# Row sums of an attention kernel by VectorE's block transpose and a spread through DRAM, in place of products with ones and reciprocals in PSUM

## The chip, the cores and the metric

The kernel runs on one core of a Trainium2 chip. The metric is the device time of the whole kernel in microseconds, lower is better; the time before is the median of three runs.

## The reference

One transformer block on 2048 tokens of width 128, in float32: layer norm with a conditioned scale and shift, attention of 16 heads of width 64 over all 2048 positions of a head, a second norm, and a mixture of 8 experts (top 2) with a shared one. The change touches the attention alone:

```python
xq = jnp.einsum('bsh,oh->bso', x, wq)       # and xk, xv
xq = xq.reshape(bsz, N_HEADS, seqlen, HEAD_DIM)
scores = jnp.einsum('bhid,bhjd->bhij', xq, xk) * SCALE
scores = jax.nn.softmax(scores, axis=-1)
out = jnp.einsum('bhij,bhjd->bhid', scores, xv)
out = out.reshape(bsz, seqlen, N_HEADS * HEAD_DIM)
return jnp.einsum('bso,ho->bsh', out, wo)
```

The reshape is plain, so each head reads 128 tokens and has 2048 positions of its own. The softmax needs the sum of the exponentials of each row, which is what the change computes in another way.

## The kernel before

**Units.** A unit is one head and one half of its 2048 query positions (`HALF` = 1024); there are 32 (`UNITS`), halves 0 and 1 of each head in turn. In a unit the scores stand transposed, keys on the partitions and 1024 queries on the columns, one tile of 128 keys at a time, 16 tiles (`kt`). TensorE makes a tile's scores in two PSUM banks (six products, `scores`, L1342 to L1348), ScalarE turns them into exponentials in one of 8 buffers `probs` (L918), TensorE multiplies these with the values (`weigh`, L1366) into one bank, and POOL adds the exponentials of all tiles (`add`, L1003, L1009) in two chains, `acc` and `acc_odd`, 14 additions of 128x1024, and merges the two in a fifteenth (L995). The total still has to be summed over its 128 partitions, for each of 1024 queries.

**Peaks.** The softmax subtracts for each query block a shift, from the maxima of products made ahead of time: for each unit 16 pairs (`pair`, L1289 on TensorE) are made while an earlier unit runs. All go to the same two PSUM banks (6 and 7), one after another, and TensorE waits for `peak_free` before each. VectorE reduces a pair to its maxima from PSUM (L1079), but for pairs 1, 3, ... 13 (`TAKEN`): these ScalarE copies to `peak_copy` (L860) and VectorE reduces the copy two places later (L1089). Then a small product turns the maxima (`turn_shift`), VectorE keeps them (L1097), and SyncE sends them by DMA (L742).

**The order by hand.** A unit has 8 steps of 4 places, so 32 places. In each step places 0 and 1 are the scores of two tiles, places 2 and 3 the value products of two earlier ones. Behind each place every engine runs the jobs that `side_jobs` puts there, in the same order on each engine: the next head's projections (`LONG_JOBS`: q, k, v), their remainders (`LOW_PLACES`), pairs 4 to 15 at places 1, 3, ... 23 (so pair 10 at place 13 and pair 11 at place 15) and pairs 0 to 3 of a later unit at places 25 to 31. Each engine's queue is served in order.

**Row sums and scaling.** "sum" (place 6 in half 0, 10 in half 1): two products of ones with the total, in the job bank (`sum_unit`, L1379), give each query's sum on all 64 partitions of a head. "inv": four reciprocals of 128 columns, PSUM to PSUM (`invert`, L1105). "scale": `scale_outputs` (L1112) multiplies the values' product `o_raw` (ScalarE's copy, L870) with them into `oT`. "out" (half 0, place 22): the head's output projection (`project`, L1392) and the residual sum on VectorE (`add_head`, L1118). The last unit's sum is made in the experts' part (`LAST_SUM`).

**SyncE's queue** holds, in a unit of half 0, the DMAs that swap the two 64-partition halves of `k_hi` behind each k (places 14 and 18), those of the differences behind "low k" (places 16 and 20) and the shift's (place 26); in half 1 the shift's alone.

**The end.** At places 17 and 27 to 31 of the last head, VectorE makes the remainders of expert weights from two SBUF tensors (L1178) and small steps of the norm (L366, L582, L583); the experts follow.

## Time and profile before

| | |
|---|---|
| median of three runs | 1318.63 us |
| the profiled execution's time | 1317.36 us |
| its span | 1315.6 us |
| TensorE busy | 1297.5 us, 99% |
| POOL busy | 1176.0 us, 89% |
| VectorE busy | 911.3 us, 69% |
| ScalarE busy | 888.3 us, 68% |
| granted TensorE clock | 0.999 |

The span runs from the first to the last instruction of one execution; the execution's own time is a little longer. A busy TensorE is not one at its peak, since the ends of its matmuls are modelled. The shares are means over attention (about 44 to 1228 us) and the experts behind it.

### The profile page before, as it was taken

To read this page: it belongs to the slowest core of one execution; us is meant where nothing else is said; L and a number is where in the kernel's file an instruction comes from. 1 tells how busy PE (TensorE), PEld (TensorE's weight loads), DVE (VectorE), ACT (ScalarE), POOL (GpSimd) and SP (SyncE) were. 2 spreads that over 40 slices of the span, in tenths; PEclk is the share of its full clock that TensorE was granted. 3 is DMA by queue.
4 is the path that set the end of the run, shared out by engine and by line. 5 is a ranking of instruction groups with operands and counts; after the bars stand their busy time and mean duration, and the time that the engine had idled before them with its cause. 6 is when DMAs were issued, how large, how long until landed. Compare 5 with 4: busy or idle time off the path is not lost. (4 is left out here: it accounts for less than half of the span.)

```text
span 1315.6 us, 22284 instructions
## 1 busy us (share of the span) xinstructions
PE 1297.5 (99%) x8792; PEld 705.3 (54%) x8792; DVE 911.3 (69%) x1036; ACT 888.3 (68%) x1096; POOL 1176.0 (89%) x538
## 2 busy tenths in 40 slices
PE   7999999999999999999999999999999999999998
PEld 5545545454555545454555555454545545454787
DVE  6767667676767677677767676776767676859575
ACT  6666767676766766666766666676767667775474
POOL 2499999999999999999999999999999999999644
PEclk9999999999999999999999999999999999999999
DMA  8010202020110202020100202020200102001323
GB/s 210 11 39 1 49 1 49 1 49 1 27 24 1 49 1 49 1 49 1 38 13 1 49 1 49 2 49 0 49 1 10 40 1 49 1 1 30 101 73 89
DMA packets 31962, 41.55 MB, mean 32 GB/s; under 512 B 4298, under 2 KB 15186, under 8 KB 31858
## 3 DMA queue, kind: packets, MB, share of 16 engines
q1 hardware_dynamic: 31714, 40.13, 12.5%
q8 instruction: 69, 1.13, 0.4%
q14 instruction: 35, 0.29, 0.1%
q10 hardware_dynamic: 144, 0.00, 0.0%
HBM read 13.70 MB, written 1.11 MB: 11 GB/s over the span
## 5 line engine op out<-in xcount | busy, mean ns | idle before, releaser
L918 ACT ACTIVATE probs<-ps 128x1024 f32<-128x1024 f32 x512 | 498.7, 1032 | 78.7 <-PE ps L1348 75.9
L1079 DVE TENSOR_REDUCE peak_parts<-ps 128x2 f32<-128x1024 f32 x297 | 362.2, 1223 | 236.8 <-PE ps L1289 235.1
L1366 PE MATMUL ps<-probs,v_sb 128*64 128x512 f32 x2048 | 522.8, 606 | 0.0
L1009 POOL TENSOR_TENSOR acc<-acc,probs 128x1024 f32<-128x1024 f32 x192 | 457.7, 2384 | 31.2 <-ACT probs L918 29.6
L1009 POOL TENSOR_TENSOR acc_odd<-acc_odd,probs 128x1024 f32<-128x1024 f32 x192 | 459.5, 2393 | 0.0
L860 ACT COPY peak_copy<-ps 128x1024 f32<-128x1024 f32 x215 | 218.6, 1017 | 242.0 <-PE ps L1289 168.0
L1089 DVE TENSOR_REDUCE peak_parts<-peak_copy 128x2 f32<-128x1024 f32 x215 | 260.7, 1212 | 34.2 <-ACT peak_copy L860 34.2
L1366 PEld LDWEIGHTS ps<-probs,v_sb 128*64 128x64 f32 x2048 | 123.8, 136 | 157.3 <-issue 118.4
L1342 PE MATMUL ps<-q_hi,d_swap_hi 64*128 64x512 f32 x512 | 201.4, 393 | 0.4 <-ACT probs L918 0.4
L1342 PE MATMUL ps<-q_hi,d_hi 64*128 64x512 f32 x512 | 201.5, 394 | 0.0
L1348 PE MATMUL ps<-q_hi,d_swap_lo 64*128 64x512 f32 x512 | 200.7, 392 | 0.0
L1348 PE MATMUL ps<-q_hi,d_lo 64*128 64x512 f32 x512 | 200.7, 392 | 0.0
L1345 PE MATMUL ps<-q_lo,d_hi 64*128 64x512 f32 x512 | 199.8, 390 | 0.0
L1345 PE MATMUL ps<-q_lo,d_swap_hi 64*128 64x512 f32 x512 | 199.7, 390 | 0.0
L1289 PE MATMUL ps<-k_hi,q_hi 64*128 64x512 f32 x512 | 120.3, 466 | 2.7 <-DVE peak_parts L1079 2.6
L1289 PE MATMUL ps<-k_swap_hi,q_hi 64*128 64x512 f32 x512 | 117.4, 454 | 1.3 <-DVE peak_parts L1079 1.1
L1289 PEld LDWEIGHTS ps<-k_hi,q_hi 64*128 64x128 f32 x512 | 47.7, 183 | 129.4 <-DVE peak_parts L1079 65.7
L1289 PEld LDWEIGHTS ps<-k_swap_hi,q_hi 64*128 64x128 f32 x512 | 47.6, 183 | 125.4 <-DVE peak_parts L1079 54.4
L1105 DVE RECIPROCAL ps<-ps 128x128 f32<-128x128 f32 x128 | 113.3, 930 | 0.0
L1345 PEld LDWEIGHTS ps<-q_lo,d_hi 64*128 64x128 f32 x512 | 94.7, 185 | 13.2
L1342 PEld LDWEIGHTS ps<-q_hi,d_swap_hi 64*128 64x128 f32 x512 | 95.0, 186 | 11.1 <-ACT probs L918 0.9
L1348 PEld LDWEIGHTS ps<-q_hi,d_lo 64*128 64x128 f32 x512 | 94.5, 185 | 11.7
(237 smaller groups left out, 1571.6 us busy)
## 6 DMA issues: line engine op xcount, KB each, us to landing
k_swap_hi<-k_hi SPq DMA_DIRECT2D x64, 128.0 KB, 2.3
d_swap_hi<-d_hi SPq DMA_DIRECT2D x64, 128.0 KB, 2.3
d_swap_lo<-d_lo SPq DMA_DIRECT2D x64, 128.0 KB, 2.3
q_hi<-weights_dram SPq DMA_DIRECT2D x8, 256.0 KB, 3.2
q_lo<-weights_dram SPq DMA_DIRECT2D x8, 256.0 KB, 4.6
k_hi<-weights_dram SPq DMA_DIRECT2D x8, 256.0 KB, 5.9
k_swap_hi<-weights_dram SPq DMA_DIRECT2D x8, 256.0 KB, 5.3
probs<-in_L_ffn_w_dram SPq DMA_DIRECT2D x2, 512.0 KB, 5.9
```

What stands on the lines that cost most here:

```text
L860: act.copy(peak_copy[:, :, :], ps[:, PEAK_BANK:PEAK_BANK + 2, :]).then_inc(peak_free, 1)
L918: act.activation(probs[:, kt % PROBS, :], ps[:, 2 * place:2 * place + 2, :].rearrange("p a b -> p (a b)"), ACT.Exp, scale=SCALE).then_inc( ...
L1009: pool.tensor_tensor(total, total, probs[:, kt % PROBS, :], ALU.add).then_inc(added, 1)
L1079: dve.tensor_reduce(peak_parts[:, :, i // STRETCHES, i % STRETCHES], ps[:, bank:bank + 2, :], AX.X, ALU.max).then_inc(peak_free, 1)
L1089: dve.tensor_reduce(peak_parts[:, :, i // STRETCHES, i % STRETCHES], peak_copy[:, :, :], AX.X, ALU.max).then_inc(copy_read, 1)
L1105: dve.reciprocal(job.ps[:, cols], job.ps[:, cols]).then_inc(part_inverted, 1)
L1289: mm = pe.matmul(ps[:, bank + b, :], q_hi[at, target_parity, q:q + P], keys[at, target_parity, cols], start=True, stop=True, tile_position ...
L1342: pe.matmul(ps[:, slot + b, :], hi[b][at[b], p, cols], q_hi[at[b], p, q], start=kt < 2, stop=False, tile_position=(b * HEAD_DIM, 0), skip_ ...
L1345: pe.matmul(ps[:, slot + b, :], hi[b][at[b], p, cols], q_lo[at[b], p, q], start=False, stop=False, tile_position=(b * HEAD_DIM, 0), skip_g ...
L1348: mm = pe.matmul(ps[:, slot + b, :], lo[b][at[b], p, cols], q_hi[at[b], p, q], start=False, stop=kt >= 2, tile_position=(b * HEAD_DIM, 0), ...
L1366: mm = pe.matmul(ps[at:at + HEAD_DIM, PV_BANK, :], v_sb[:, p, chunk_of(kt) * HEAD_DIM:(chunk_of(kt) + 1) * HEAD_DIM], probs[:, kt % PROBS, ...
```

## The change

The products with ones and the PSUM reciprocals go, but for the last unit. In their place, for each unit done, at places of the next unit that are the same in both halves:

- place 8, "turn sum": VectorE transposes the total (128x1024) in blocks of 32x32 into `k_raw`;
- place 10, "add sum": it sums over 32 neighbouring columns, 128x1024 to 128x32 (`sum_parts`): now each of four partition groups holds the part of its 32 keys rows for all 1024 queries;
- place 12, "fold": a block transpose of 128x32, four copies that bring the four groups to 32 partitions, a reduction over the four, a reciprocal of 32x32;
- SyncE (`spread_sums`, in its queue at place 12) writes the 1024 reciprocals to DRAM, waits until they have landed, and reads them back with two DMAs that repeat a row on 64 partitions;
- place 20 (28 in the last unit), "scale": VectorE multiplies `o_raw` with them, both in SBUF.

The scratch for it is the unit's own `acc` half. "out" moves from place 22 of half 0 to place 14 of half 1. New waits: ScalarE before its copy into `k_raw` (`sums_added`) and before its copy of the values' product (`out_scaled`), POOL before the first addition of a unit and TensorE before the projection (`out_scaled`), VectorE before the scaling (`sums_spread`). The diff, with one line of context at each place; left out are the lines that allocate `sum_parts` and the six semaphores.

```diff
@@ -39,8 +39,8 @@
 LONG_JOBS = (
-    {2: ("q", 0), 6: ("sum", 0), 14: ("k", 0), 18: ("k", 1), 22: ("out", 0), 26: ("shift", 0)},
-    {2: ("q", 1), 6: ("v", 0), 10: ("sum", 0), 19: ("v", 1), 26: ("shift", 0)},
+    {2: ("q", 0), 14: ("k", 0), 18: ("k", 1), 26: ("shift", 0)},
+    {2: ("q", 1), 6: ("v", 0), 14: ("out", 0), 19: ("v", 1), 26: ("shift", 0)},
 )
@@ -48,13 +48,11 @@
 INVERSES = 4
-SCALE_PLACES = (
-    {6: ("inv", 0), 7: ("inv", 1), 8: ("inv", 2), 10: ("inv", 3), 11: ("scale", 0)},
-    {11: ("inv", 0), 12: ("inv", 1), 13: ("inv", 2), 15: ("inv", 3), 16: ("scale", 0)},
-)
-
-COUNTED = ("q", "k", "v", "sum", "shift")
-JOBS_PER_HEAD = 10
+SUM_PLACES = {8: ("turn sum", 0), 10: ("add sum", 0), 12: ("fold", 0)}
+SCALE_PLACE, LATE_SCALE_PLACE = 20, 28
+
+COUNTED = ("q", "k", "v", "shift")
+JOBS_PER_HEAD = 8
 
@@ -81,11 +79,11 @@
 
-def side_jobs(half, sums=True, project=True, pairs=True, early=True, last_head=False, before_last=False):
+def side_jobs(half, sums=True, outs=True, project=True, pairs=True, early=True, last_head=False, before_last=False):
 
     for place, (kind, i) in LONG_JOBS[half].items():
-        if sums if kind in ("sum", "out") else pairs if kind == "shift" else project:
+        if outs if kind == "out" else pairs if kind == "shift" else project:
             places[place].append((kind, i))
@@ -102,8 +100,9 @@
     if sums:
-        for place, job in SCALE_PLACES[half].items():
+        for place, job in SUM_PLACES.items():
             places[place].append(job)
+        places[LATE_SCALE_PLACE if last_head and half == 1 else SCALE_PLACE].append(("scale", 0))
     if before_last:
@@ -236,7 +238,7 @@
         def jobs_at(t):
-            return PROLOGUE_JOBS if isinstance(t, int) and t == 0 else t * (2 * JOBS_PER_HEAD) + (PROLOGUE_JOBS - 1)
+            return t * (2 * JOBS_PER_HEAD) + PROLOGUE_JOBS
 
@@ -276,7 +278,8 @@
                     final_head = last and p == 1
-                    plan = side_jobs(half, sums=not (first and p == 0 and half == 0), project=not final_head,
+                    plan = side_jobs(half, sums=not (first and p == 0 and half == 0), outs=not (first and p == 0),
+                                     project=not final_head,
                                      pairs=not (final_head and half == 1), early=not final_head,
@@ -305,6 +308,19 @@
         TAIL_PAIRED = 7
+
+        sums_dram = nc.dram_tensor("sums_dram", [2, HALF], F32, kind="Internal").ap()
+
+        class SumParts:
+
+            def __init__(self, unit_done):
+                total = acc[:, unit_done % 2, :]
+                self.turned = k_raw[:, P:P + HALF]
+                self.spread = total[:, 0:BANK]
+                self.parts_turned = total[:, BANK:BANK + 32]
+                self.quarters = total[0:32, BANK + 128:BANK + 256].rearrange("p (g i) -> p g i", g=4)
+                self.sums = total[0:32, BANK + 256:BANK + 288]
+                self.inverse = total[0:32, BANK + 288:BANK + 320]
 
@@ -744,6 +760,17 @@
 
+            def spread_sums(unit_done):
+
+                parts = SumParts(unit_done)
+                sp.wait_ge(sums_inverted, unit_done + 1)
+                row = sums_dram[unit_done % 2:unit_done % 2 + 1, :]
+                sp.dma_start(row.rearrange("a (j i) -> (a j) i", j=32), parts.inverse).then_inc(sums_out, 16)
+                sp.wait_ge(sums_out, 16 * (unit_done + 1))
+                for b in range(2):
+                    sp.dma_start(parts.spread[b * HEAD_DIM:(b + 1) * HEAD_DIM, :],
+                                 row[:, b * BANK:(b + 1) * BANK].broadcast_to([HEAD_DIM, BANK])).then_inc(sums_spread, 16)
+
             def swap(parity, i, src, dst, signal):
@@ -779,6 +806,8 @@
                             for kind, i in jobs:
+                                if kind == "fold":
+                                    spread_sums(unit - 1)
                                 if kind == "k":
@@ -829,13 +858,15 @@
                 keep_setup(n)
-            def side(job, kind, i, parity):
+            def side(job, kind, i, parity, sums_before=0):
 
                     if kind == "k":
+                        if sums_before:
+                            act.wait_ge(sums_added, sums_before)
                         act.copy(k_raw[:, P + i * BANK:P + (i + 1) * BANK], job.ps).then_inc(raw_ready, 1)
@@ -860,13 +891,10 @@
 
-            sums = []
-
-            def copy_pv(unit_done, sum_before):
+            def copy_pv(unit_done):
                 act.wait_ge(pv_done, PAIRS * unit_done)
-                if sum_before is not None:
-
-                    act.wait_ge(job_free, sum_before)
+                if unit_done > 1:
+                    act.wait_ge(out_scaled, unit_done - 1)
                 act.copy(o_raw[:, :], ps[:, PV_BANK, :]).then_inc(o_copied, 1)
@@ -921,14 +949,12 @@
                                 if kind in COUNTED:
-                                    side(Job(jobs_at(t) + local), kind, i, 1 - p)
+                                    side(Job(jobs_at(t) + local), kind, i, 1 - p, unit)
                                 if kind == "step k":
                                     take_pair(i, target * PEAK_PAIRS + i, target)
-                                if kind == "sum":
-                                    sums.append(jobs_at(t) + local + 1)
                                 if kind in ("turn", "logits", "weights"):
@@ -943,10 +969,10 @@
                         if step == 0 and not first:
-                            copy_pv(unit, sums[-1] if sums else None)
+                            copy_pv(unit)
 
             pairs_of_heads(body)
-            copy_pv(UNITS, sums[-1])
+            copy_pv(UNITS)
             ffn_act(act)
@@ -997,8 +1023,9 @@
                     pool.wait_ge(exped, unit * TILES + (kt + 2))
+                    if n == 1 and unit > 1:
+                        pool.wait_ge(out_scaled, unit - 1)
                     if n == 2 and unit > 0:
-
                         pool.wait_ge(added, unit * ADDS)
@@ -1107,9 +1134,39 @@
 
-                dve.wait_ge(part_inverted, unit_done * INVERSES)
+                dve.wait_ge(part_inverted, INVERSES)
                 dve.wait_ge(o_copied, unit_done)
                 dve.tensor_tensor(oT[:, half_done, :], o_raw[:, :], job.ps, ALU.mult).then_inc(job_free, 1)
+
+            def turn_sum(unit_done, half_done):
+
+                dve.wait_ge(added, unit_done * ADDS + ADDS)
+                dve.transpose(SumParts(unit_done).turned, acc[:, half_done, :]).then_inc(sums_turned, 1)
+
+            def add_sum(unit_done):
+
+                parts = SumParts(unit_done)
+                dve.wait_ge(sums_turned, unit_done + 1)
+                dve.tensor_reduce(sum_parts[:, :], parts.turned.rearrange("p (j r) -> p j r", r=32), AX.X,
+                                  ALU.add).then_inc(sums_added, 1)
+
+            def fold_sums(unit_done):
+
+                parts = SumParts(unit_done)
+                dve.wait_ge(sums_added, unit_done + 1)
+                link(dve.transpose(parts.parts_turned, sum_parts[:, :]))
+                for g in range(4):
+                    ins = dve.tensor_copy(parts.quarters[:, g, :], parts.parts_turned[32 * g:32 * g + 32, :])
+                link(ins)
+                link(dve.tensor_reduce(parts.sums, parts.quarters.rearrange("p g i -> p i g"), AX.X, ALU.add))
+                dve.reciprocal(parts.inverse, parts.sums).then_inc(sums_inverted, 1)
+
+            def scale_unit(unit_done, half_done):
+
+                dve.wait_ge(sums_spread, 32 * (unit_done + 1))
+                dve.wait_ge(o_copied, unit_done + 1)
+                dve.tensor_tensor(oT[:, half_done, :], o_raw[:, :], SumParts(unit_done).spread,
+                                  ALU.mult).then_inc(out_scaled, 1)
 
@@ -1160,10 +1217,14 @@
                                     low_k(Job(jobs_at(t) + (local - 1)), i, 1 - p, head * 2 + (3 + i))
-                                if kind == "inv":
-                                    invert(i, Job(jobs_at(t) + (local - 1)))
+                                if kind == "turn sum":
+                                    turn_sum(unit - 1, 1 - half)
+                                if kind == "add sum":
+                                    add_sum(unit - 1)
+                                if kind == "fold":
+                                    fold_sums(unit - 1)
                                 if kind == "scale":
-                                    scale_outputs(Job(jobs_at(t) + (local - 1)), unit, 1 - half)
+                                    scale_unit(unit - 1, 1 - half)
                                 if kind == "out":
@@ -1385,6 +1446,7 @@
                 pe.wait_ge(job_free, job.earlier)
+                pe.wait_ge(out_scaled, min(2 * head + 2, UNITS - 1))
                 for half in range(2):
@@ -1451,8 +1513,6 @@
                                     pair(i, (unit + 2) * PEAK_PAIRS + i, head + 1, 1 - p, half, PEAK_BANK)
-                                if kind == "sum":
-                                    sum_unit(job, unit - 1, 1 - half)
                                 if kind == "out":
```

## Rows read from the trace of the kernel before

**Rows 1.** The page, part 1: busy us (share of the span) xinstructions:

```profile
PE 1297.5 (99%) x8792; PEld 705.3 (54%) x8792; DVE 911.3 (69%) x1036; ACT 888.3 (68%) x1096; POOL 1176.0 (89%) x538
```

**Rows 2.** Busy time by stretch, two units of attention:

```profile
core 0: us, PE busy (x) PEld busy (x) DVE busy (x) ACT busy (x) POOL busy (x), PEclk, DMA share, GB/s
154.00:228.00 74.00, 74.00 (x516) 38.52 (x514) 50.85 (x53) 50.95 (x60) 71.07 (x32) 1.00 0.10 22
```

**Rows 3.** Groups by line: busy us, mean ns of one, idle before:

```profile
L860 ACT COPY peak_copy<-ps 128x1024 f32<-128x1024 f32 x215 | 218.6, 1017 | 242.0 <-PE ps L1289 168.0 <-DVE peak_parts L1089 74.0
...
L1105 DVE RECIPROCAL ps<-ps 128x128 f32<-128x128 f32 x128 | 113.3, 930 | 0.0
...
L1379 PE MATMUL ps<-acc,ones 128*64 128x512 f32 x128 | 32.9, 593 | 0.0
...
L1112 DVE TENSOR_TENSOR oT<-o_raw,ps 128x512 f32<-128x512 f32 x32 | 22.0, 687 | 1.1
```

**Rows 4.** Waits: engine line, waited for: us in total, times, longest:

```profile
PEld ps L1289 <- DVE peak_parts L1079: 120.1, 166, 1.9
```

**Rows 5.** Timeline of TensorE in a unit of half 1 (start us, us):

```profile
533.77 1.03 PE L1379 MATMUL ps<-acc,ones 128*64 128x512 f32 x4
534.63 1.03 PE L1366 MATMUL ps<-probs,v_sb 128*64 128x512 f32 x4
...
537.31 0.40 PE L1289 MATMUL ps<-k_swap_hi,q_hi 64*128 64x512 f32 x2
...
539.50 0.51 PE L1289 MATMUL ps<-k_swap_hi,q_hi 64*128 64x512 f32 x2
```

**Rows 6.** Timeline of VectorE, same unit:

```profile
534.12 1.21 DVE L1089 TENSOR_REDUCE peak_parts<-peak_copy 128x2 f32<-128x1024 f32 x1
535.24 1.77 DVE L1105 RECIPROCAL ps<-ps 128x128 f32<-128x128 f32 x2
```

**Rows 7.** Timeline of POOL, same unit:

```profile
535.70 2.40 POOL L1009 TENSOR_TENSOR acc_odd<-acc_odd,probs 128x1024 f32<-128x1024 f32 x1
538.15 2.38 POOL L1009 TENSOR_TENSOR acc<-acc,probs 128x1024 f32<-128x1024 f32 x1
540.47 2.40 POOL L1009 TENSOR_TENSOR acc_odd<-acc_odd,probs 128x1024 f32<-128x1024 f32 x1
```

**Rows 8.** Timelines of VectorE and POOL at the norm's small steps:

```profile
1141.79 0.21 DVE L366 RECIPROCAL rstd<-std 128x12 f32<-128x12 f32 x1
...
1142.03 0.62 DVE L582 TENSOR_TENSOR shift_ln<-mean_var,rstd 128x12 f32<-128x12 f32 x1
...
1142.56 2.42 POOL L1009 TENSOR_TENSOR acc_odd<-acc_odd,probs 128x1024 f32<-128x1024 f32 x1
...
1142.69 2.33 DVE L583 TENSOR_SCALAR shift_ln<-shift_ln 128x12 f32<-128x12 f32 x1
```

**Rows 9.** Timeline of VectorE and POOL at the weight remainders:

```profile
1182.86 7.58 DVE L1178 TENSOR_TENSOR w_lo<-w1T,k_hi 128x384 fp32r<-128x384 f32 x3 [5.31 <-ACT k_hi L938]
...
1190.11 2.55 POOL L1003 TENSOR_TENSOR acc<-probs 128x1024 f32<-128x1024 f32 x1
1190.36 2.45 DVE L1178 TENSOR_TENSOR w_lo<-w1T,shared_hi 128x128 fp32r<-128x128 f32 x1
...
1192.73 0.68 DVE L576 TENSOR_TENSOR d_hi<-hT,d_hi 128x512 fp32r<-128x512 f32 x1
```

**Rows 10.** Timeline of TensorE in a unit of half 0:

```profile
502.00 0.50 PE L1289 MATMUL ps<-k_swap_hi,q_hi 64*128 64x512 f32 x2
...
509.76 1.92 PE L1392 MATMUL ps<-wo,oT 128*64 128x128 f32 x32
511.51 1.03 PE L1366 MATMUL ps<-probs,v_sb 128*64 128x512 f32 x4
```

**Rows 11.** DMA issues: xcount, KB each, median us to landing:

```profile
k_swap_hi<-k_hi SPq DMA_DIRECT2D x64, 128.0 KB, 2.3
...
q_hi<-weights_dram SPq DMA_DIRECT2D x8, 256.0 KB, 3.2
```

More of the change, by code:

```diff
@@ L156, in build @@
         acc_odd = sb("acc_odd", [P, HALF])
+        sum_parts = sb("sum_parts", [P, 32])
         oT = sb("oT", [P, 2, BANK])
@@ L228, in build @@
         part_inverted = sem("part_inverted")
+        sums_turned, sums_added, sums_inverted = sem("sums_turned"), sem("sums_added"), sem("sums_inverted")
+        sums_out, sums_spread, out_scaled = sem("sums_out"), sem("sums_spread"), sem("out_scaled")
         out_full, mid_ready = sem("out_full"), sem("mid_ready")
```

## The prediction

> **What bounds the kernel now.** I read the busy shares first. TensorE is busy 99% of the span, POOL 89%, VectorE 69% [rows 1]. Busy matmuls are modelled, so the share alone proves little; a stretch of two attention units is needed beside it. In 74.00 us (two units, one half of the queries each, so 37.0 us for one) TensorE has no gap, at a granted clock of 1.00, and POOL works 71.07 us [rows 2]. So two engines are nearly full: TensorE wholly, and POOL all but 1.5 us per unit. VectorE has 11 us to spare per unit, but it is no free engine: all peak products go through one pair of PSUM banks, and `pair` on TensorE waits for the release of the pair before. The table of waits has TensorE's weight loads waiting 120.1 us in total, 166 times and at most 1.9 us, for VectorE's peak reduction [rows 4]. Now those waits are short, and other queued matmuls cover them. The reader should keep one thing in mind: a block of several us on VectorE between two peak reductions stops TensorE.
>
> **What the change removes.** On TensorE, the ones product of each unit but the last: 128 records for 32 products, 32.9 us, so 1.03 us each [rows 3]; in the order of time it takes from 533.77 to the next start at 534.63, 0.86 us, because neighbours overlap [rows 5]. 31 of them are gone: at most 27 to 32 us. On VectorE, four reciprocals of 0.93 us, 3.7 us per unit, in pieces of 0.9 to 2.6 us [rows 3, 6]. Also gone is the PSUM operand of the scaling (0.69 us [rows 3]); both its operands now lie in SBUF.
>
> **What it adds on VectorE, per unit, in queue order.** Place 8: a block transpose of 128x1024. The trace has no transpose; the nearest rows are reductions of the same 1024 columns, 1.21 us [rows 6]. I take 1.2 us, with 0.7 and 2.5 as ends. It falls into the idle time before the peak reduction at place 9 and costs nothing; without that cover it would cost its length. Place 10: a reduction of 1024 columns from SBUF, 1.2 us. Place 12: the fold, in one run: a 32-column transpose (0.2), four SBUF to SBUF copies of 32x32, a small reduction (0.3), a reciprocal of 32 columns (between 0.21 for 12 columns and 0.93 for 128 [rows 3, 8], so 0.3). Place 20: the scaling. By the widths alone this is 1.2 + 1.2 + 1.4 + 0.7 = 4.5 us against 4.4 us removed, an even exchange. The widths alone are not the cost.
>
> **The disputed cost: SBUF work of VectorE while POOL adds.** Near the end of attention VectorE does three tiny steps on 12 columns while POOL adds [rows 8]. The reciprocal takes 0.21 us. The product of two SBUF tensors takes 0.62 us and ends at 1142.65, as POOL goes over to its next addition (1142.56). The tensor_scalar from SBUF to SBUF starts at 1142.69 and takes 2.33 us: it ends at 1145.02, when that POOL addition ends (1142.56 + 2.42 = 1144.98). The weight remainders say the same of several in a row: three L1178 with both inputs in SBUF take 7.58 us, and a following one of only 128 columns 2.45 us, one addition of POOL each (that from 1190.11 on, for the last); 2 us later, with POOL idle, 512 columns of the same form take 0.68 us [rows 9]. So some forms wait until POOL's current addition is over, POOL starts its next before VectorE's next of these gets in, and each pays a whole addition. Reductions from SBUF don't: 1.21 us beside a busy POOL [rows 6]. The two-input scaling is of the waiting form by these rows. An SBUF to SBUF copy isn't in the trace; it is bounded by 0.1 us (as the reciprocal, it doesn't wait) and 2.4 us (as the tensor_scalar, also one SBUF input and an SBUF output). I take the tensor_scalar's side: it is the only one-input elementwise row of that kind besides the reciprocal, and the reciprocal is the slow exception in rate as well.
>
> The Trainium skill, "SBUF — State Buffer", section Who interferes with whom, states this outright: copy, cast and tensor_scalar from SBUF to SBUF can take VectorE's second port pair, which is GpSimd's only one, and whoever comes second waits for the whole instruction; tensor_reduce never does. The rows on tensor_scalar and on reductions agree; for the copy no run here shows it yet. By that page the four copies are blocked as in my sum; with the reciprocal's price instead the sum would be that of the first rival below.
>
> **The sum, in a unit of half 1.** Before the change VectorE ends the reduction at place 9 at 535.24 [rows 6], and TensorE gets to the pairs of places 13 and 15 at 537.31 and 539.50 [rows 5]. After it: add sum 535.2 to 536.4, small transpose to 536.6. POOL's additions start at 535.70, 538.15 and 540.47, and the last of these ends at 542.87 [rows 7]. Copy 1 gets in at 538.1, copy 2 at 540.5, copy 3 at 542.8. Copy 4 depends on whether POOL has more work. The addition from 540.47 is that of tile 7, the last tile scored before place 15; TensorE stands still there, because the pair of place 15 waits for the reduction of that of place 13, which stands behind the fold. So POOL has run dry and copy 4 goes at 542.9. Reduction, reciprocal and their semaphores: 543.6. Peak reduction 1.2: 544.8. The pair that went at 539.50 goes at 544.8: 5.3 us late. The saved ones product doesn't reduce this (TensorE comes to the gate earlier and waits longer), and the projection that now stands at place 14 is hidden in it. What is late next: ScalarE's copy of the pair of place 15 waits for `peak_copy`, which VectorE frees 1.2 us later; ScalarE needs 1.0 us [rows 3], TensorE meanwhile 1.4 us of scores: 0.8 us more. The scaling at place 20 waits for a POOL addition (0 to 2.3, mean 1.2) and 0.7 us for itself; most of it goes into VectorE's slack, 0.3 us is charged. Half 1: 6.4 us.
>
> **Half 0.** The same block before the pair that now goes at 502.00 [rows 10], 5.3 us, with 0.3 us behind it (the k product at place 14 fills part of the wait, and so the later copy costs less) and 0.3 us for the scaling. The projection at place 22, which takes TensorE from 509.76 to 511.51, is gone here: 1.75 us back [rows 10]. Half 0: 4.1 us.
>
> Pairs follow the fold in units 1 to 30, 15 of each half; unit 31 has no peak products, there TensorE gives 0.86 us and gets the 1.75 us projection: 1 us. Sum: 15 x 6.4 + 15 x 4.1 + 1 = 158 us. The profiled execution took 1317.36 us, 1.8 us over its span, and lies 1.3 us under the median of 1318.63. So 1317.4 + 158 = 1475 us; against the median it is 1477, and I write 1475.
>
> **Edits that I cost at nothing.** The way through DRAM: write 4 KB, wait, read two broadcasts of 128 KB. The nearest rows are the swaps of 128 KB, 2.3 us to landing, and the broadcasts of token weights, 3.2 us and more when eight go together [rows 11]. With about 2 us for the write that is 5 to 8 us after the reciprocal: 548.6 to 551.6, and VectorE comes to place 20 at about 551. If it is later than that, VectorE waits with the next peak reductions behind it, and what exceeds about 1 us reaches TensorE. On SP's queue the swaps of k_hi (half 0, places 14 and 18) and of the differences (16 and 20) stand behind the wait for the write, some 6 us late, and are needed from place 29 and from the next unit: covered by 10 us. The shift's DMA at place 26 comes after all. POOL's new wait for `out_scaled` asks for a scaling of the unit before: long done. ScalarE's new waits (`sums_added` before k_raw, `out_scaled` before o_raw) ask for steps at place 10 and in the earlier unit: done when reached. The end of the kernel keeps its ones product.
>
> **Rivals.**
> First, faster or unchanged: the copies don't wait for POOL. Then the fold ends at 538.1, the next peak reduction at 539.3, before TensorE needs it with the projection in front of it, and each unit gains the 0.86 us: 27 us, 1291 us. But POOL must do 15 additions at 2.34 us start to start, 35.1 us, and loses up to 0.6 us to the scaling, so of the 36.1 us that would remain hardly anything is free; it may give back 0.3 us per unit. 1291 to 1303 us. For it speaks that no row has a copy; against it the tensor_scalar row. It decides if a copy takes under 0.3 us beside a busy POOL.
> Second, about unchanged: one wait lets all four copies through. The fold ends at 539.4, the peak reduction at 540.6: half 1 loses 1.1 us, half 0 gains 0.7, scaling 0.3 each: +15 us, 1333 us (1320 to 1360). Against it: the last two L1178 have no wait between them and each took a whole addition [rows 9].
> Third, much slower: the transposes wait for POOL too, or the spread lands late. A block of 1.2 to 2.4 us more at places 8 and 12, or 2 to 3 us at place 20: 2.5 us more per unit, +75 us, 1550 us and up to 1640. For it: no row has a transpose, and the slack at place 20 is small.
>
> **Chances and range.** Forecast 0.68, with its own range from one copy fewer that waits (2.3 us less per unit, 1405 us) to a worse phase with copy 4 blocked too (2.3 us more, 1545 us). First rival 0.10, second 0.10, third 0.12. The range 1360 to 1570 us leaves out the first two rivals but for a rest, and the greater part of the third's upper half. A difference under 2% (26 us) cannot be told from none with this kernel's measurement. Slower than 1345 us: 0.68 + 0.12 + 0.04. Faster than 1292 us: 0.04, the better half of the first rival. Within: 0.12.
>
> **What would show it.** Right: the 32x32 copies of the fold take about 1.2, 2.4, 2.4 and 0.2 us while their neighbours take 0.2 to 0.3; TensorE has one gap of 5 to 7 us in each unit, before the pair of place 15, released by the peak reduction; POOL's share falls to about 80%, TensorE's too. Wrong: copies of 0.1 us; POOL at 97% between merges and no gap on TensorE. If transposes take over 2 us with POOL busy, or VectorE idles before the scaling for the DMA, the third rival has a part. The forecast fails in size first by the number of copies that find POOL busy.

## The result and the profile after

The changed kernel takes 1516.82 us (median of four, 1514.95 to 1517.97) against 1318.96 us: a ratio of 1.150, 95% interval 1.148 to 1.152. It is slower by 198 us. One of the four executions of the kernel before took 1810.67 us, the other three 1318.17 to 1319.29. The changed kernel's profiled execution took 1515.69 us, its span is 1513.9 us, 198.3 more than before. The forecast was 1475 us, +158.

The page of the changed kernel, part 1, answers to [rows 1]:

```profile
PE 1330.7 (88%) x8668; PEld 730.0 (48%) x8668; DVE 1109.7 (73%) x1191; ACT 889.3 (59%) x1096; POOL 1176.7 (78%) x538
```

POOL has the same work as before (1176.0 and 1176.7 us) and TensorE 124 matmuls fewer, yet both have lost eleven points of share: both wait. VectorE is 198 us busier. Its groups by line answer to [rows 3]:

```profile
L1159 DVE COPY acc<-acc 32x32 f32<-32x32 f32 x124 | 190.1, 1533 | 2.3
L1168 DVE TENSOR_TENSOR oT<-o_raw,acc 128x512 f32<-128x512 f32 x31 | 46.9, 1512 | 3.2 <-DMA acc<-sums_dram 3.2
L1144 DVE STREAM_TRANSPOSE k_raw<-acc 128x1024 f32<-128x1024 f32 x31 | 38.3, 1235 | 0.0
L1150 DVE TENSOR_REDUCE sum_parts<-k_raw 128x32 f32<-128x1024 f32 x31 | 37.5, 1210 | 0.0
...
L1161 DVE TENSOR_REDUCE acc<-acc 32x32 f32<-32x128 f32 x31 | 11.1, 356 | 1.1
L1162 DVE RECIPROCAL acc<-acc 32x32 f32<-32x32 f32 x31 | 10.6, 341 | 1.1
...
L1157 DVE STREAM_TRANSPOSE acc<-sum_parts 128x32 f32<-128x32 f32 x31 | 6.5, 211 | 1.1
```

The seven lines of the new row sums are to be read against their widths. 124 copies of 32 columns take 1.53 us on average, more than a transpose or a reduction of 1024 columns; the reductions, the transposes and the reciprocal take what their widths ask. The table of waits follows. The waits of its first three rows came to 120.1 [rows 4], 74.0 and 29.6 us before the change:

```profile
PEld ps L1350 <- DVE peak_parts L1106: 318.4, 209, 7.4
ACT peak_copy L891 <- DVE peak_parts L1116: 292.6, 105, 7.7
POOL acc L1036 <- ACT probs L946: 232.6, 79, 7.7
...
PE ps L1350 <- DVE peak_parts L1106: 162.3, 65, 6.5
```

TensorE, ScalarE and POOL all wait for peak reductions, directly or through one another. Where, the timeline of a unit of half 0 shows (all engines, cut to the fold; it answers to [rows 5 to 7]):

```profile
570.78 2.39 POOL L1036 TENSOR_TENSOR acc_odd<-acc_odd,probs 128x1024 f32<-128x1024 f32 x1
...
571.64 6.36 DVE L1159 COPY acc<-acc 32x32 f32<-32x32 f32 x4
...
573.12 2.37 POOL L1036 TENSOR_TENSOR acc<-acc,probs 128x1024 f32<-128x1024 f32 x1
...
575.42 2.36 POOL L1036 TENSOR_TENSOR acc_odd<-acc_odd,probs 128x1024 f32<-128x1024 f32 x1
...
578.70 1.15 DVE L1106 TENSOR_REDUCE peak_parts<-ps 128x2 f32<-128x1024 f32 x1
...
579.90 0.72 PE L1350 MATMUL ps<-k_swap_hi,q_hi 64*128 64x512 f32 x2 [5.26 <-DVE peak_parts L1106]
```

VectorE starts the four copies at 571.64 and is through at 578.00. In this time POOL does the additions that end at 573.17, 575.49 and 577.78. Behind the fold stands the reduction of the pair of place 13, behind that, on TensorE, the pair of place 15: 5.26 us idle. And this is what the prediction did not have: the busy time by stretch from the gap on. The clock that TensorE is granted, as a share of full speed, is the figure behind POOL's.

```profile
core 0: us, PE busy (x) PEld busy (x) DVE busy (x) ACT busy (x) POOL busy (x), PEclk, DMA share, GB/s
574.60:579.90 5.30, 0.04 (x2) 0.00 (x0) 5.20 (x7) 0.30 (x1) 3.19 (x2) 1.00 0.01 1
579.90:582.00 2.10, 2.10 (x10) 1.73 (x12) 1.67 (x2) 0.94 (x2) 0.00 (x0) 0.53 0.13 49
582.00:584.00 2.00, 2.00 (x11) 0.90 (x11) 1.07 (x2) 2.00 (x4) 0.44 (x1) 0.64 0.79 227
584.00:586.00 2.00, 2.00 (x24) 1.16 (x20) 1.98 (x2) 0.89 (x3) 2.00 (x2) 1.00 0.90 208
```

TensorE stood idle for 5.26 us, still at the full clock. When it starts again it gets 0.53 and 0.64 of it, which is 1.2 GHz for most of the 4.1 us to 584; in the stretch from 584 on it is back at 2.4 GHz. The first pair takes 0.72 us where [rows 5] has 0.51.

The length of a unit is read from POOL's merges (the addition that joins the two chains), one in each unit, 31 intervals from the first start to the last; before, then after:

```profile
L995 POOL TENSOR_TENSOR acc<-acc,acc_odd x32: 2368/2392/2543, 84.3 to 1226.6; 128x1024 f32<-128x1024 f32 x32
```

```profile
L1021 POOL TENSOR_TENSOR acc<-acc,acc_odd x32: 2372/2390/2544, 86.3 to 1422.2; 128x1024 f32<-128x1024 f32 x32
```

(1226.6 - 84.3) / 31 = 36.85 us became (1422.2 - 86.3) / 31 = 43.09 us, +6.24 us per unit or 194 of the 198 us. The forecast had +5.1 (158 over 31).

### The profile page after: what moved, and what is told of

Read it like the earlier page. It is cut to its first block and busy times, and to the rows that moved or that the text cites. A ratio compares the mean times of both kernels' runs of the same rounds, so it can differ in the third digit from the quotient of the medians.

```text
span 1513.9 us, 22313 instructions
## 1 busy us (share of the span) xinstructions
PE 1330.7 (88%) x8668; PEld 730.0 (48%) x8668; DVE 1109.7 (73%) x1191; ACT 889.3 (59%) x1096; POOL 1176.7 (78%) x538
## 3 DMA queue, kind: packets, MB, share of 16 engines
HBM read 21.83 MB, written 1.24 MB: 15 GB/s over the span
## 5 line engine op out<-in xcount | busy, mean ns | idle before, releaser
L1403 PE MATMUL ps<-q_hi,d_hi 64*128 64x512 f32 x512 | 214.6, 419 | 6.5 <-ACT probs L946 6.5
L1403 PE MATMUL ps<-q_hi,d_swap_hi 64*128 64x512 f32 x512 | 214.6, 419 | 0.4 <-ACT probs L946 0.4
L1406 PE MATMUL ps<-q_lo,d_hi 64*128 64x512 f32 x512 | 214.2, 418 | 0.0
L1406 PE MATMUL ps<-q_lo,d_swap_hi 64*128 64x512 f32 x512 | 214.1, 418 | 0.0
L1409 PE MATMUL ps<-q_hi,d_lo 64*128 64x512 f32 x512 | 214.0, 418 | 0.0
L1409 PE MATMUL ps<-q_hi,d_swap_lo 64*128 64x512 f32 x512 | 213.9, 418 | 0.0
L1159 DVE COPY acc<-acc 32x32 f32<-32x32 f32 x124 | 190.1, 1533 | 2.3
L1350 PEld LDWEIGHTS ps<-k_hi,q_hi 64*128 64x128 f32 x512 | 51.7, 199 | 132.7 <-DVE peak_parts L1106 71.3
L1409 PEld LDWEIGHTS ps<-q_hi,d_lo 64*128 64x128 f32 x512 | 103.0, 201 | 12.8
L1409 PEld LDWEIGHTS ps<-q_hi,d_swap_lo 64*128 64x128 f32 x512 | 103.0, 201 | 12.4
L1406 PEld LDWEIGHTS ps<-q_lo,d_hi 64*128 64x128 f32 x512 | 102.3, 200 | 13.3
```

Of the source, the lines that this page charges most:

```text
L1159: ins = dve.tensor_copy(parts.quarters[:, g, :], parts.parts_turned[32 * g:32 * g + 32, :])
L1350: mm = pe.matmul(ps[:, bank + b, :], q_hi[at, target_parity, q:q + P], keys[at, target_parity, cols], start=True, stop=True, tile_position ...
L1403: pe.matmul(ps[:, slot + b, :], hi[b][at[b], p, cols], q_hi[at[b], p, q], start=kt < 2, stop=False, tile_position=(b * HEAD_DIM, 0), skip_ ...
L1406: pe.matmul(ps[:, slot + b, :], hi[b][at[b], p, cols], q_lo[at[b], p, q], start=False, stop=False, tile_position=(b * HEAD_DIM, 0), skip_g ...
L1409: mm = pe.matmul(ps[:, slot + b, :], lo[b][at[b], p, cols], q_hi[at[b], p, q], start=False, stop=kt >= 2, tile_position=(b * HEAD_DIM, 0), ...
```

## The experiments

Each run is compared with runs of the kernel before on the same chip (1317 to 1319 us).

**1. Copies replaced by reductions of length one.** In the changed kernel:

```diff
-    ins = dve.tensor_copy(parts.quarters[:, g, :], parts.parts_turned[32 * g:32 * g + 32, :])
+    ins = dve.tensor_reduce(parts.quarters[:, g, :], parts.parts_turned[32 * g:32 * g + 32, :, None], AX.X, ALU.add)
```

> The four 32x32 copies of the fold become tensor_reduce over an axis of length one, same data, same places; nothing else changes. Theory (the copies wait for POOL's addition, the block on VectorE stops TensorE at the pair of place 15): each takes 0.1 to 0.2 us beside a busy POOL, the fold's four fall from 6.3 us to under 0.8, the gap of 5.3 us on TensorE shrinks to under 1 us, the granted clock goes back to about 1.00, and the time to 1290 to 1335 us. Rival 1 (the way through DRAM, the scaling or the new waits carry the loss): the time stays above 1450 us. Rival 2 (any four instructions across partition groups are slow on VectorE): the moves stay over 1 us each and so does the time.

Measured: 1329.43 us, ratio 1.007 (1.005 to 1.010). The four moves are one line:

```profile
L1159 DVE TENSOR_REDUCE acc<-acc 32x32 f32<-32x32 f32 x124 | 21.7, 175 | 2.3
```

The moves take 0.175 us each where the copies took 1.53; same data, same partitions, same place, same trip through DRAM, and 187 us are gone. From 500 to 580 us TensorE now waits for peak reductions 1.1 us in all, 0.7 at the longest, where the changed kernel waits 10.4 and 5.3. Both rivals fall: neither the trip nor the waits nor moves across partition groups cost anything near it.

**2. One copy left**, g = 0, the other three as reductions.

> Only the first of the four moves stays a copy, the other three are reductions. Theory: the one copy pays the rest of one addition, about 1.2 us (0 to 2.4) as the first did; TensorE's gap is 1 to 2 us, the time 1310 to 1360 us, 10 to 45 us over the run without copies. If the number of copies didn't matter (one block whatever the count), the time would be near 1515 us.

Measured: 1362.04 us, ratio 1.033 (1.029 to 1.038), 33 us over run 1. The one copy takes 1.67 us on average (51.7 us over 31). The time (two executions, 1357.6 and 1366.5) is 2 us above the stated 1360. The count matters: one copy costs 33 us, four 187.

**3. The kernel before, with four copies.** Row sums by ones products as they were; at place 12, in both halves:

```diff
+        places[12].append(("moves", 0))
+                                if kind == "moves":
+                                    for g in range(4):
+                                        dve.tensor_copy(moved[:, g, :], spare[32 * g:32 * g + 32, :])
```

> The kernel before, with row sums by ones products as they were, and four useless 32x32 copies from SBUF to SBUF on VectorE at place 12 of each unit (their result is not used). Theory: the copies take 5 to 8 us in sum beside POOL's additions, TensorE stops at the pair of place 15, 4 to 6 us per unit: 1318 + 120 to 200 = 1440 to 1520 us with a granted clock near 0.95. Rival (the loss needs the rest of the change: DRAM, SP's queue, scaling): under 1345 us.

Measured: 1505.33 us, ratio 1.142 (1.140 to 1.144), granted clock 0.96. The copies by line (duration ns min/median/max), then by total:

```profile
L1171 DVE COPY moved<-spare x124: 169/2232/2327, 96.6 to 1390.8; 32x32 f32<-32x32 f32 x124
```

```profile
L1171 DVE COPY moved<-spare 32x32 f32<-32x32 f32 x124 | 186.2, 1501 | 1.3
```

Here nothing else of the change is present: no trip through DRAM, no new wait, no moved projection, and the ones products are still made. The copies alone bring 188 us of loss.

**4. The copies spread out**: copy 1 at place 12, the others at 14, 16 and 18, the rest of the fold at 19, the scaling at 27.

```diff
-SUM_PLACES = {8: ("turn sum", 0), 10: ("add sum", 0), 12: ("fold", 0)}
-SCALE_PLACE, LATE_SCALE_PLACE = 20, 28
+SUM_PLACES = {8: ("turn sum", 0), 10: ("add sum", 0), 12: ("move", 0), 14: ("move", 1), 16: ("move", 2),
+              18: ("move", 3), 19: ("fold", 0)}
+SCALE_PLACE, LATE_SCALE_PLACE = 27, 28
```

> The changed kernel with the fold cut up: the small transpose and copy 1 at place 12, copies 2, 3 and 4 at places 14, 16 and 18, the rest of the fold at 19, the scaling at 27 (28 in the last unit). As many copies, and each can still wait for a whole addition. Theory (it is the unbroken block in front of one peak reduction that stops TensorE, VectorE's total still fits): the wait is cut into pieces of 1.2 to 2.4 us with peak reductions between them, TensorE's gaps fall to under 2 us each, and the time is 1360 to 1440 us, though the copies together still take 5 to 9 us. If only the sum of the waits counted, the time would be 1500 us or more.

Measured: 1401.91 us, ratio 1.064 (1.062 to 1.066).

```profile
L1160 DVE COPY acc<-acc 32x32 f32<-32x32 f32 x124 | 173.8, 1402 | 3.6
```

The copies wait nearly as long as in one block (173.8 us against 190.1), but the kernel is 115 us faster. In the stretch from 500 to 580 us TensorE has gaps of 0.47, 0.37, 1.86, 2.20 and 0.37 us in place of one of 4 to 5 per unit; the 1.86 are a wait for another product of VectorE (`d_lo`), the others for peak reductions. This run also moves the scaling; in run 7 below such a move, in half 0 alone, is worth 11 us, so it is not what brings the 115. So the waits of VectorE cost by their place, not by their sum.

**5. The write to DRAM made twice** in the changed kernel:

```diff
+                sp.dma_start(row.rearrange("a (j i) -> (a j) i", j=32), parts.inverse).then_inc(sums_out, 16)
+                sp.wait_ge(sums_out, 32 * (unit_done + 1))
```

> The changed kernel with the write to DRAM and the wait for it made twice in each unit, about 2 us more between the reciprocal and the scaling. Prediction's claim: the trip ends near the moment when VectorE comes to place 20, with 1 us or so to spare. From the trace after, the only scaling that waits for the DMA is that of the last unit (3.2 us). So 0 to 1.5 us per unit: the time within 0 to 45 us above 1517, and a wait of the scaling for the DMA appears in VectorE's rows. If it is well hidden: within 5 us of 1517.

Measured: 1516.89 us, ratio 1.151 (1.150 to 1.153), where the change had 1.150 (1.148 to 1.152): no difference, the case that I had called well hidden. Of the scalings only two wait for the DMA, 5.0 us in all (one, 3.2 us, in the changed kernel). The DMA rows of the changed kernel (KB each, us to landing) show why:

```profile
acc<-sums_dram SPq DMA_DIRECT2D x62, 128.0 KB, 2.9
...
sums_dram<-acc SPq DMA_DIRECT2D x31, 4.0 KB, 1.3
```

The write takes 1.3 us and the broadcasts 2.9 us. With the time to issue them that is about 5 us from the reciprocal, at the lower end of what the prediction took. The second write adds 1.3 us and is still hidden.

**6. TensorE kept busy in the gap.** In the changed kernel, before the pair of place 15; the stationary operand is zero, so the score bank keeps what it holds:

```diff
+            def keep_busy(unit):
+                pe.wait_ge(exped, unit * TILES + 7)
+                for _ in range(5):
+                    pe.matmul(ps[:, 0, :], k_raw[:, 0:P], wqT[:, 0:BANK], start=False, stop=False, skip_group_check=True)
```

> The changed kernel, and before the pair of place 15 in each unit but the first five products of zeros (128x128 by 512 columns, about 0.9 us each), added to a score bank that they leave as it is: TensorE works through most of the gap of 4.2 to 5.3 us in place of idling. Theory on the part that the prediction missed (after the gap TensorE runs at half clock for 2.5 to 3 us, 0.53 to 0.64 granted, some 1.3 us lost per unit): the granted clock is 1.00 and the time falls by 25 to 45 us, to 1470 to 1492 us. Rival (the missing 40 us come from something else, such as VectorE's backlog behind the fold): the time stays within 8 us of 1517 or grows.

Measured: 1485.37 us, ratio 1.127 (1.125 to 1.129), granted clock 0.995 (0.953 without). More work on the engine that sets the end makes the kernel 31 us faster. POOL's merges:

```profile
L1021 POOL TENSOR_TENSOR acc<-acc,acc_odd x32: 2369/2392/2418, 85.5 to 1392.8; 128x1024 f32<-128x1024 f32 x32
```

(1392.8 - 85.5) / 31 = 42.17 us per unit, 0.92 us less than the changed kernel; against before it is +5.32. The pair of place 15 still waits for the same reduction, so what comes back is speed behind the gap and not the gap itself.

**7 and 8. Repairs on run 1.** Run 7 does the scaling of half 0 at place 28. Run 8 does, besides, all steps of places 8 to 12 at place 4 in the last unit.

```diff
-        places[LATE_SCALE_PLACE if last_head and half == 1 else SCALE_PLACE].append(("scale", 0))
+        places[LATE_SCALE_PLACE if last_head or half == 0 else SCALE_PLACE].append(("scale", 0))
...
-            places[place].append(job)
+            places[4 if last_head and half == 1 else place].append(job)
```

> The kernel with reductions in place of copies (1329 us), and the scaling in units of half 0 at place 28 instead of 20. There VectorE has 2.6 us idle, while at place 20 the gaps of 0.7 and 0.4 us on TensorE follow. Theory: both gaps go, 15 units by up to 1.1 us, but POOL is busy 71.9 of 74.0 us, so it gives at most half: 1310 to 1325 us. If the gaps come back at another pair: 1325 to 1335.

> As the run before it, and in the last unit the steps at places 8, 10 and 12 all stand at place 4, ahead of the gating of the experts. There SyncE's queue made the write of the experts' weights wait behind the trip of the sums, and ScalarE's next copy waited 6.1 us for it, with TensorE 4.0 us behind. Theory: 3 to 5 us less than the run before it, 1305 to 1321 us, about the time of the kernel before or just under it. If the queue on SyncE wasn't the reason: no difference.

Measured: 1318.34 us, ratio 1.0006 (0.9996 to 1.0016), and 1316.04 us, ratio 0.9988 (0.9975 to 1.0001). Run 7 is 11 us under run 1, as expected. Run 8 is 2.3 us under run 7, less than the 3 to 5 expected, with intervals that overlap: its gain is not settled. The wait that it aims at is seen in the two traces, though (timeline of ScalarE in the last unit, run 1 and run 8, idle time in brackets):

```profile
1226.52 0.57 ACT L543 COPY wqT<-ps 8x512 f32<-8x512 f32 x1 [6.11 <-DMA weights_dram<-wqT]
```

```profile
1206.00 0.57 ACT L543 COPY wqT<-ps 8x512 f32<-8x512 f32 x1 [0.69 <-DMA weights_dram<-wqT]
```

In run 1, SyncE's queue holds the experts' weights (ready at 1219.9) behind its wait for the sums' write, and ScalarE, which needs the buffer, stands still for 6.1 us. Run 8 has 0.7 us there, though ScalarE now waits 5.2 us for a small product of TensorE two copies earlier. Run 8 is the fastest of the versions that compute the whole result, and it cannot be told from the kernel before.

**9 and 10. POOL relieved.** Run 8 and the kernel before, each with two of POOL's additions per unit cut to one column. Both leave the exponentials of two of the sixteen key tiles out of the row sums, so they serve to measure time only:

```diff
+                    cols = slice(0, 1) if n in (4, 9) else slice(0, HALF)
-                    pool.tensor_tensor(total, total, probs[:, kt % PROBS, :], ALU.add).then_inc(added, 1)
+                    pool.tensor_tensor(total[:, cols], total[:, cols], probs[:, kt % PROBS, cols], ALU.add).then_inc(added, 1)
```

> The last version (reductions, scaling late, last unit mended; 1316 us) with two of POOL's fifteen additions per unit narrowed to one column, so that POOL has 4.7 us less work in a unit and its share falls from 98% to about 85%. Leaves out of the row sums the exponentials of two of the sixteen key tiles. Theory: POOL is now what holds back the 0.86 us that TensorE saved; relieved, the unit goes from 36.3 us to 35.9 or below, and the time by 8 to 20 us, to 1296 to 1308 us. Rival (VectorE or TensorE itself holds it): 1312 to 1318 us.

> The kernel before with the same two additions of POOL per unit narrowed to one column (the same two tiles are left out of the row sums). Theory: it is held by TensorE, with POOL idle 1.5 us per unit, so it gains little: 1308 to 1318 us. The distance between this run and the one before it is then what the ones products are worth without POOL, 10 to 22 us (0.86 us for each of 31 products, less what start and end cost). Rival (POOL holds the kernel before as well): it falls as far as the other and the two are within 4 us.

Measured: 1308.71 us, ratio 0.9934 (0.9922 to 0.9946), and 1317.95 us, ratio 0.9997 (0.9988 to 1.0006). The second is as expected: the kernel before gains nothing from a relieved POOL. The first falls by 7 us against run 8, just short of its range, and its trace does not bear my theory out where it matters. Busy time in two units of run 8, then of run 9:

```profile
core 0: us, PE busy (x) PEld busy (x) DVE busy (x) ACT busy (x) POOL busy (x), PEclk, DMA share, GB/s
500.00:574.00 74.00, 73.56 (x514) 38.56 (x510) 54.55 (x65) 51.26 (x60) 72.71 (x32) 1.00 0.12 30
```

```profile
500.00:574.00 74.00, 73.50 (x508) 37.94 (x507) 52.84 (x65) 51.73 (x62) 63.63 (x31) 1.00 0.13 34
```

and the merges of run 8, then of run 9:

```profile
L1021 POOL TENSOR_TENSOR acc<-acc,acc_odd x32: 2381/2401/2426, 86.6 to 1222.4; 128x1024 f32<-128x1024 f32 x32
```

```profile
L1021 POOL TENSOR_TENSOR acc<-acc,acc_odd x32: 2367/2370/2546, 83.9 to 1215.2; 128x1024 f32<-128x1024 f32 x32
```

POOL goes from 72.71 to 63.63 us of 74.00, TensorE stays at 73.5. In the middle of the run two units take 72.63 us in run 8 (merges at 522.37 and 595.00) and 72.68 in run 9 (519.53 and 592.21): the same. The whole 31 intervals take (1222.4 - 86.6) = 1135.8 and (1215.2 - 83.9) = 1131.3 us, and 3.9 of these 4.5 us are the last interval alone (42.5 against 38.6); the first merge is 2.7 us earlier. So the 7 us are at the two ends, and POOL is not what takes the saved time in a steady unit, full as it is.

## Why the prediction was right, and where its size was off

**The mechanism: as forecast, shown.** The step on which all hung was which price a 32x32 copy from SBUF to SBUF has beside a busy POOL, 0.1 or 2.4 us; the trace of before had no such copy, and I took the side of the tensor_scalar [rows 8]. The four copies of the row above end one by one: the trace's single records have 1.56, 2.30, 2.28 and 0.17 us. Copies 1 to 3 end just behind POOL's three additions, copy 4 is free, since POOL had run dry; in sum 6.36 us against the 6.3 us of the forecast (536.6 to 542.9). Runs 1 and 3 take the copies out and put them in alone: 1329 and 1505 us. That it is POOL they wait for is read from these ends and from copy 4; no run has the copies with POOL's additions taken away.

The Trainium skill, "SBUF — State Buffer", section Who interferes with whom, has copies in a two-port mode contend with GpSimd, and tensor_reduce never. Run 1 agrees (1.53 us for a copy against 0.175 us for the reduction of the same 32x32).

**The rivals.** First (copies don't wait) and second (one wait lets all through) are refuted by the same records. Run 1 is nearly what the first rival described, and gives 1329 where I wrote 1291 to 1303: that price was too good by 26 us or more. One part is VectorE's scaling in half 0 (11 us, run 7). Another is that of the 0.86 us of a ones product a steady unit of run 8 gets only 0.46 (36.77 to 36.31 us, merges 524.31 and 597.84 against 522.37 and 595.00), 12 us over the units. Of the missing 0.40, 0.22 us is idle time of TensorE (73.56 of 74.00), the rest has no row that I can name; POOL, my guess, is excluded by run 9. The third part is at the end of attention: the last three merge intervals take 114.2 us before, 127.7 in run 1 (whose profiled execution, 1335.32 us, is the slowest of its four) and 118.5 in run 8.

That last part also says why run 8 is no faster than before. Between its profile and that of before, the first 28 intervals are 10.8 us shorter; the last three are 4.3 us longer, the first merge is 2.3 us later and what stands behind the last merge 2.5 us longer.

The third rival (transposes wait, or the trip is late) is refuted: 1.24 us for 1024 columns and 0.21 us for 32, and run 5.

**The block in front of the peak reduction.** The forecast had the pair of place 15 go 5.3 us late in both halves. Counted from the first exponential of its unit, it goes 22.48 us in, in place of 17.18, in half 1: 5.3 us late, as forecast. In half 0 it is 21.71 in place of 17.12, 4.6 us late. The idle time of TensorE is another measure: 5.26 us in half 0 (above), and in half 1, in the next unit, 4.23 us, because the projection at place 14 takes up part of it:

```profile
616.58 1.92 PE L1454 MATMUL ps<-wo,oT 128*64 128x128 f32 x32
...
623.58 0.50 PE L1350 MATMUL ps<-k_swap_hi,q_hi 64*128 64x512 f32 x2 [4.23 <-DVE peak_parts L1106]
```

Run 4 shows that the place makes the price.

**The term that was missing: TensorE's clock.** The forecast charged the gaps alone and put their effect on the clock at nothing. The rows have 0.53 and 0.64 of the clock for 4 us after a gap, and run 6, with the gap filled, gives 31.5 us back. That run's unit is 5.32 us longer than before; the forecast had 5.1 us. So the term that was missing is this one: 31.5 of the 42 us between 1475 and 1517. About 5 more are the last unit (below), and the profiles have 2.0 us more in front of the first merge and 2.7 behind the last one.

That 5.1 fits 5.32 tests the mean, not the two halves, for which the forecast had 6.4 and 4.1 us. By the merges run 6 is 5.2 us over before in half 1 and 5.3 in half 0; from the first exponential of a unit to that of the next, 5.8 and 4.7. Either way half 1 was put too high and half 0 too low, by 0.6 to 1.2 us each. That the two cancel is luck.

The Trainium skill warns of idle gaps of TensorE between bursts, which put its clock back to half ("TensorE: Matmul & The Clock Gate", section Why this matters for your kernels). I did not weigh it, and the trace agrees: 0.53 and 0.64 behind a gap of 5.26 us.

**Ends.** The last unit was charged 1 us. Its merge interval went from 38.96 us (1187.61 to 1226.57) to 44.95 us (1377.23 to 1422.18), so 6 us. In the changed kernel ScalarE waits 8.6 us there for the DMA of the experts' weights (1.1 us before), which stands behind the wait for the sums' write on SyncE. I had looked at the DMAs behind that wait in a steady unit, and not at those of the last one.

**Costed at nothing.** The way through DRAM, the swaps behind it and the new waits of POOL, ScalarE and TensorE: in steady units the table of waits has none of them (the scaling waits once for its DMA, 3.2 us, in the last unit), and run 5 makes the write twice at no cost. This held, but for the last unit.

## What to carry to other kernels

Price a VectorE instruction by its width only after asking whether it has to wait for POOL: beside back-to-back additions of POOL, a 32x32 copy took up to a whole addition in a steady unit (2.3 us), and a reduction of length one does the same move for 0.18 us. Look at what stands behind such an instruction in its queue: nearly the same waits cost 187 us in one block before a peak reduction and 72 to 84 us spread out (1402 against 1329 in run 1 and 1318 in run 7, where the scaling is late too). And charge a gap on TensorE more than its length; here gaps of 4.2 to 5.3 us cost another 0.9 us each in clock.

## What the runs showed of the hardware that was not expected

**A waiting VectorE instruction can be passed over several times.** In [rows 8, 9] and in the fold of the changed kernel VectorE is let in at POOL's next boundary. In run 1 one scaling was not (timeline of VectorE, then of POOL):

```profile
1172.32 8.98 DVE L1168 TENSOR_TENSOR oT<-o_raw,acc 128x512 f32<-128x512 f32 x1
```

```profile
1173.77 2.39 POOL L1036 TENSOR_TENSOR acc_odd<-acc_odd,probs 128x1024 f32<-128x1024 f32 x1
1176.08 2.37 POOL L1036 TENSOR_TENSOR acc<-acc,probs 128x1024 f32<-128x1024 f32 x1
1178.38 2.37 POOL L1036 TENSOR_TENSOR acc_odd<-acc_odd,probs 128x1024 f32<-128x1024 f32 x1
1185.71 2.34 POOL L1036 TENSOR_TENSOR acc<-acc,probs 128x1024 f32<-128x1024 f32 x1 [4.96 <-ACT probs L946]
```

It starts to wait at 1172.32 and ends at 1181.30: POOL's additions of 1173.77, 1176.08 and 1178.38 all go first, and it gets in when POOL runs out of work. The other scalings of that run take 0.69 to 2.19 us. Run 7 has one of 11.51 us, and the single copy of run 2, 1.4 to 1.6 us in most units, once took 6.82. That it waits for POOL is read from these ends, and what decides which of the two goes first was not tried.

**It goes the other way too.** In the last unit of run 1 four two-input instructions of VectorE follow one another without waiting, and POOL's addition, begun at 1220.30, takes 3.79 us in place of 2.38:

```profile
1220.30 3.79 POOL L1036 TENSOR_TENSOR acc_odd<-acc_odd,probs 128x1024 f32<-128x1024 f32 x1
1220.33 1.34 DVE L1239 TENSOR_TENSOR w_lo<-w3T,k_swap_hi 128x384 fp32r<-128x384 f32 x3
1221.60 0.27 DVE L1239 TENSOR_TENSOR w_lo<-w3T,shared_hi 128x128 fp32r<-128x128 f32 x1
```

**The clock can fall in the prologue.** From 40 to 50 us the granted clock is 1.00 in the profiled run of before, 0.71 in that of the change, and 0.74 in run 10, whose prologue is that of before. The first merge is later in both, 86.3 and 85.6 us against 84.3; that the clock is the reason is not shown. So 1 to 2 us of a single profile of this kernel are no property of the change. The stretch in before, the change and run 10:

```profile
40.00:50.00 10.00, 8.15 (x61) 5.04 (x63) 8.65 (x10) 4.34 (x10) 1.01 (x1) 1.00 0.01 2
```

```profile
40.00:50.00 10.00, 8.57 (x41) 5.32 (x43) 7.39 (x10) 3.40 (x8) 0.00 (x0) 0.71 0.01 2
```

```profile
40.00:50.00 10.00, 8.39 (x41) 5.08 (x39) 7.53 (x9) 3.18 (x8) 0.00 (x0) 0.74 0.01 2
```
